# Vision tower block on one core: front half of the next sample run between the heads of the present one

## The chip, the cores and the metric

The kernel runs on one core of one Trainium2 chip. The metric is device time in microseconds (us) from one launch to its end. Before the change two runs took 6684.24 and 6710.91 us, with a median of 6697.57 us. Times in the text that carry no unit are us.

The engines are called PE (TensorE), DVE (VectorE), ACT (ScalarE), POOL (GpSimd) and SP (SyncE, which issues the transfers). PEld is TensorE's weight load. A "record" is one line of the trace; a float32 matmul leaves two records there, a float32r or bfloat16 matmul one.

## The reference, cut to what matters

32 samples, each 64 channels x 256 positions x 4; after the token mixer each is 256 rows of 256 values, and a class row is put in front (257 rows).

```python
# token mixer, per sample (q, k, v are 64x64 projections of the raw sample, per head of 4)
ew = exp(w_bias * local_mask); ek = exp(k)
y = sigmoid(q) * (ew @ (ek * v)) / (ew @ ek)
h = layernorm(y @ out_w + out_b + x) * ln_g + ln_b
# attention, 16 heads, 16 wide q and k, 64 wide v
t = layernorm(concat(cls, h))
q, k, v = l2norm(t @ Wq), l2norm(t @ Wk), l2norm(t @ Wv)      # per head
attn = square(relu(q @ k.T))
out = tanh_norm(attn @ v)                                      # tanh(|o|) * o / |o|
h = concat(cls, h) + out @ Wout
# then a latent attention and a mixture of experts over all rows (not touched by the change)
```

## The kernel before, in words

`build` runs stages one after another: `load_constants`, `mixer_and_attention` (all 32 samples), `class_tokens`, `latent_attention`, and then the experts. Only the first two change; the others take over one tile (`QT` is allocated in `latent_attention` afterwards, and not by `build`).

In `mixer_and_attention` each engine has its own program, and the programs meet at semaphores. Nothing reorders them: the order of the work is the order in which the code is written. Each engine runs a loop over the samples, and one sample goes through its stages in a row:

- **Mixer.** DVE spreads the raw sample (`tensor_copy(x2)`, line 534). PE projects it (lines 678 to 684), ACT takes exponentials, PE forms the two mixes with `ewT` (line 692), DVE takes the reciprocal of the denominator (line 545), PE adds bias, residual and output projection in bank 5 (lines 697 to 706), and DVE makes two layer norms, with the roots on POOL (`power`, line 64).
- **Projections.** PE turns the rows (line 713) and projects q and k (line 719) and v (line 725). ACT squares all of them, DVE sums the squares per head and forms reciprocal roots by Newton steps (`inverse_root`, lines 71 to 81). q and k are then scaled (line 579), split into a high and a low part (`hl`, ACT line 471, DVE and POOL line 420), turned by PE in float32r (line 737) and copied into `QT` and `KTr` (ACT line 477). A head's 16 values become 64 rows this way. v is scaled by DVE into `V` (line 601).
- **Attention.** The work goes by units: `u` is half of the keys (128) for a pair of heads. `sim(u)` (line 754) is two float32r matmuls of 64 rows that run side by side in the array, ACT takes relu (line 486), DVE multiplies relu by the raw product in PSUM (`prob`, line 614), and `values(u)` (line 764) is two float32 matmuls of 64 columns each, side by side. Once per pair the class row enters with one float32 matmul (line 814, `v.vcls_bd`), and `square_sums` (line 772) sums the squares of an output pair with two matmuls whose moving side has 8 columns.
- **Output.** Norms of the outputs, their tanh, a scale per head, which PE turns (line 780) and spreads over the rows as a high and a low part (lines 792 and 793), DVE's scaling (line 646), and the output projection (line 799, 16 float32 matmuls per sample) in bank 5; DVE adds the residual (line 670). Then SP stores the rows, and only then does DVE begin the next sample's line 534.

So PE waits for DVE and ACT in the mixer, the norms and the output, while in the attention PE is always fed.

## Time and the profile before

| what | value |
|---|---|
| runs | 6684.24 and 6710.91 us, median 6697.57 |
| profiled execution, its own time | 6671.73 us |
| span of the profiled execution | 6670.0 us |
| mean granted TensorE clock | 0.696 of full speed |
| PE busy | 77% of the span, 23484 records |
| DVE, ACT, POOL busy | 43%, 27%, 11% |
| samples' copies (line 534), 32 of them | 67.0 to 3272.6 us |

The span runs from the first to the last instruction. The first 67 us are constants; the 32 samples last to 3377 us; all behind that is code that the change leaves alone. The copies of line 534 are (3272.6 - 67.0) / 31 = 103.4 us apart. The profile is one execution; the granted clock says which part of TensorE's 2.4 GHz was granted in a stretch: 1.0 is 2.4 GHz, 0.5 is 1.2 GHz.

### The profile page before, as it was taken

How to read it: one execution, taken by the hardware profiler on the slowest of the kernel's cores; microseconds unless marked ns; L12 is line 12 of the kernel's file. 1: busy time of each engine (PE TensorE's matmuls, PEld its weight loads, DVE VectorE, ACT ScalarE, POOL GpSimd, SP SyncE). 2: the span in 40 equal slices, each digit the busy share in tenths (PEclk: the TensorE clock that was granted, in tenths of full speed). 3: DMA queues.
4: the chain of work that ended last, by engine and by line, in shares of the span. 5: the costliest groups of instructions: out<-in, count | busy, mean ns of one | idle time of the engine just before them, and what ended most of it. 6: DMA issues, size and time to landing. Idle time of an engine off the chain costs nothing. (4 is left out here: it accounts for less than half of the span.)

```text
span 6670.0 us, 76169 instructions
## 1 busy us (share of the span) xinstructions
PE 5105.2 (77%) x23484; PEld 3231.9 (48%) x23485; DVE 2858.4 (43%) x7538; ACT 1831.1 (27%) x5049; POOL 729.7 (11%) x630
## 2 busy tenths in 40 slices
PE   5888888887888878888838889889888862217887
PEld 3454454545545545445415555555555532216776
DVE  3444444444444444444415444544544542213333
ACT  1222222222222222222203333333333331002332
POOL 1000000000000000000050000000000002222333
PEclk7766766667666676676757776776766765559999
DMA  1000000000000000000000000000000021113333
GB/s 39 9 9 5 9 5 9 9 5 9 9 5 9 5 9 9 5 9 5 6 7 12 15 14 10 14 14 13 11 14 14 10 74 58 54 42 60 57 57 55
DMA packets 104402, 131.16 MB, mean 20 GB/s; under 512 B 13698, under 2 KB 84995, under 8 KB 104372
## 3 DMA queue, kind: packets, MB, share of 16 engines
q1 hardware_dynamic: 78404, 95.67, 4.8%
q0 software_dynamic: 25968, 35.15, 3.1%
q8 instruction: 12, 0.20, 0.0%
q14 instruction: 18, 0.15, 0.0%
HBM read 67.00 MB, written 63.76 MB: 20 GB/s over the span
## 5 line engine op out<-in xcount | busy, mean ns | idle before, releaser
L614 DVE TENSOR_TENSOR PR<-psA,R 128x516 f32<-128x516 f32 x512 | 352.4, 693 | 634.7 <-ACT R L486 633.8
L1155 ACT ACTIVATE m_P<-psC,m_nmax 128x129 f32<-128x129 f32 (+1 forms) x1024 | 421.2, 419 | 624.0 <-DVE m_nmax L1239 621.1
L764 PE MATMUL psA<-PR,V 128*64 128x258 f32 x2048 | 568.8, 662 | 0.9
L486 ACT ACTIVATE R<-psA 128x516 f32<-128x516 f32 x512 | 304.7, 601 | 735.8 <-PE psA L754 732.3
L1347 PE MATMUL psC<-ident,m_P 128*128 128x128 f32 x1536 | 402.6, 391 | 68.5 <-ACT m_P L1155 68.5
L1232 DVE COPY m_PT<-psC 128x256 f32<-128x256 f32 (+1 forms) x512 | 284.6, 556 | 391.2 <-PE psC L1347 390.8
L1359 PE MATMUL psC<-m_PT,m_V 128*16 128x128 f32 x3072 | 360.0, 359 | 12.5 <-DVE m_PT L1232 12.5
L799 PE MATMUL psA<-wout,OT 128*128 128x256 f32 x1024 | 362.8, 531 | 0.0
L1347 PEld LDWEIGHTS psC<-ident,m_P 128*128 128x128 f32 x1536 | 226.0, 189 | 239.2 <-ACT m_P L1155 124.6
L64 POOL TENSOR_TENSOR rstd<-rstd,inv_root 128x2 f32<-128x2 f32 x64 | 44.5, 695 | 2601.3 <-DVE rstd L528 2601.3
L1656 PE MATMUL psR<-identd,d_tn 128*128 128x128 f32 x130 | 31.1, 426 | 387.9 <-DVE d_tn L1583 387.9
L1239 DVE TENSOR_REDUCE m_nmax<-psC 128x2 f32<-128x258 f32 (+1 forms) x512 | 285.0, 557 | 96.3 <-PE psC L1335 89.5
L754 PEld LDWEIGHTS psA<-QT,KTr 64*128 64x128 f32 x1024 | 143.2, 283 | 356.8 <-issue 305.3
L814 PE MATMUL psA<-pcl,vcls_bd 16*128 16x258 f32 x512 | 309.5, 704 | 4.9 <-DVE pcl L609 4.6
L799 PEld LDWEIGHTS psA<-wout,OT 128*128 128x128 f32 x1024 | 279.7, 280 | 63.8
L754 PE MATMUL psA<-QT,KTr 64*128 64x258 f32 x1024 | 285.4, 565 | 1.3 <-DVE V L601 1.3
L772 PEld LDWEIGHTS psA<-kmask,osq 128*128 128x128 f32 x1024 | 236.9, 321 | 74.8 <-issue 74.8
L764 PEld LDWEIGHTS psA<-PR,V 128*64 128x64 f32 x2048 | 156.0, 205 | 230.1 <-issue 119.7
L1793 POOL DMA_INDIRECT out_rows<-e_y,e_dest x137 | 212.1, 1548 | 449.6 <-DVE e_y L1852 233.0
L772 PE MATMUL psA<-kmask,osq 128*128 128x8 f32 x1024 | 261.2, 366 | 0.0
L1331 PE MATMUL psC<-m_KT,QT 64*128 64x130 f32 (+1 forms) x1024 | 243.9, 474 | 0.0
L737 PE MATMUL psA<-ident_r,hl 128*128 128x128 f32 x1024 | 127.9, 312 | 132.3 <-DVE hl L420 132.3
(369 smaller groups left out, 9258.9 us busy)
## 6 DMA issues: line engine op xcount, KB each, us to landing
e_x<-xg SPq DMA_DIRECT2D x143, 129.0 KB, 2.5
xraw<-in_x SPq DMA_DIRECT2D x64, 256.0 KB, 3.8
d_x<-xs SPq DMA_DIRECT2D x13, 640.0 KB, 4.4
hs<-h SPq DMA_DIRECT2D x32, 256.0 KB, 2.0
m_h<-hs SPq DMA_DIRECT2D x32, 256.0 KB, 2.7
xs<-m_x SPq DMA_DIRECT2D x32, 256.0 KB, 2.2
out_rows<-m_base SPq DMA_DIRECT2D x32, 256.0 KB, 2.4
w_stage<-in_w SPq DMA_DIRECT2D x16, 512.0 KB, 4.9
```

The source lines that it names most:

```text
L486: act.activation(R[:, h % 2], ps[:, b:b + 2, 0:QCOLS], ACT.Relu).then_inc(relu_done, 1)
L614: dve.tensor_tensor(PR[:, h % 3], ps[:, b:b + 2, 0:QCOLS], R[:, h % 2], ALU.mult).then_inc(prob_done, 1)
L754: last = pe.matmul(ps[:, 2 * (u % 2) + hh, 0:QCOLS], KTr[rows, pr, t * P:(t + 1) * P], v.QT[rows, pr, :], start=True, stop=True)
L764: last = pe.matmul(ps[64 * hh:64 * hh + 64, 4 + pr % 2, 0:QCOLS], V[:, t, h * DV:(h + 1) * DV], PR[:, u % 3, hh, :], start=False, stop=Tru ...
L772: last = pe.matmul(ps[:, 6 + pr // 4, t * 8:t * 8 + 8], osq[:, pr % 2, t * P:(t + 1) * P], v.kmask[:, pr % 4, 0:8], start=pr % 4 == 0 and ...
L799: last = pe.matmul(ps[:, 5, t * MODEL:(t + 1) * MODEL], OT[:, pr, t * P:(t + 1) * P], v.wout[:, pr, :], start=pr == 0 and t == 0, stop=pr ...
L814: pe.matmul(ps[:, 4 + pr % 2, 0:QCOLS], v.vcls_bd[:, pr * P:(pr + 1) * P], pcl[:], start=True, stop=False, skip_group_check=True)
L1155: act.activation(PM[:, u % 2, hh, 0:N - 1], ps[:, b + hh, 0:N - 1], ACT.Exp, bias=nmax[:, t, h:h + 1], accum_out=esum[:, t, h:h + 1]).then ...
L1232: dve.tensor_copy(PT[:, u % 2, 0:n], ps[:, 4 + u % 2, 0:n]).then_inc(pT_copied, 1)
L1239: dve.tensor_reduce(nmax[:, t, 2 * hp:2 * hp + 2], ps[:, b:b + 2, 0:KEYS[t] - 1], AX.X, ALU.max, negate=True).then_inc(max_done, 1)
L1347: last = pe.transpose(ps[:, 4 + u % 2, c:c + P], PM[:, u % 2, hh, 1 + jt * P:1 + (jt + 1) * P], v.ident[:])
L1359: pe.matmul(ps[rows, 6 + g // 2, g % 2 * L + t * P:g % 2 * L + (t + 1) * P], V[:, jt, h * DK:(h + 1) * DK], PT[:, u % 2, c:c + P], start=F ...
```

## The change

It has two halves, and is made in `load_constants`, `mixer_and_attention` and the place where tiles are allocated.

**Order.** Each engine's program is now written as functions per step, and one body `sample(i, d, before, more)` runs the attention of sample i, with the mixer and projections of sample i + 1 (`more`) and the output part of sample i - 1 (`before`) between its eight pairs of heads. The loop holds two bodies, since tiles are kept twice (`d` is 0 or 1). `front(0)` runs the mixer and projections of the first sample alone, and `last` the output of the last.

**Arithmetic.** q and k stay as projected. PE writes them turned (weights stationary, tokens moving, line 971), ACT copies them to `qT` and `kT`, and `sim` becomes four float32 matmuls of 32 rows and 256 columns per pair of heads. The rows of a head are chosen by a parity mask in the copy of k. A key's norm goes into the scale of its value row (`vc = vrn * rk`, on POOL), a query's norm into the norm of the output. Gone are `hl`, its turns (line 737), the Newton roots, and the multiply with the class key (line 744). New are small matmuls for the norm sums of q and k and for the class row (`class_products`, `query_sums`). Roots of v and of the outputs are now POOL's `power` on 16 and 32 columns, and POOL scales v. `prob` squares relu's result, which lies in SBUF, and takes one instruction per pair of heads, as relu does. `square_sums` works with 2 columns. The scale's high and low part go into one matmul of 48 rows, the class row into one float32r matmul of 80 rows.

The core of the diff:

```diff
+            def sim(i, d, p):
+                c, m, g = p // 4, p // 2 % 2, p % 2
...
+                need(pe, relu_done, PAIRS * i + p)
+                for t in range(LT):
+                    for hh in range(2):
+                        rows = slice(32 * (2 * g + hh), 32 * (2 * g + hh) + 32)
+                        last = pe.matmul(ps[:, hh, t * L:(t + 1) * L], kT[rows, d, m, c, t * P:(t + 1) * P],
+                                         qT[rows, d, c, :], start=True, stop=True, skip_group_check=True)
+                last.then_inc(sim_done, 1)
...
+            def attend(i, d, p):
+                if p == 0:
+                    pe.wait_ge(p_ready, i + 1)
+                    pe.wait_ge(v_ready, 2 * i + 2)
+                need(pe, ss_done, PAIRS * i + p - 1)
+                pe.wait_ge(prob_done, PAIRS * i + p + 1)
+                pe.matmul(ps[:, 2 + p % 2, 0:QCOLS], v.vcls3[:, p * P:(p + 1) * P], v.pcl[:, d, :], start=True,
+                          stop=False, skip_group_check=True)
...
+            def prob(i, d, p):
+                dve.wait_ge(relu_done, PAIRS * i + p + 1)
+                need(dve, av_done, PAIRS * i + p - 1)
+                dve.wait_ge(acl_done, i + 1)
+                dve.tensor_copy(PR[:, p % 2, :, :, L],
+                                acl[:, d, :, 2 * p:2 * p + 2].rearrange("p t h -> p h t"))
+                dve.tensor_tensor(PR[:, p % 2, :, :, 0:L], R[:, p % 2], R[:, p % 2], ALU.mult).then_inc(prob_done, 1)
...
+            def value_rows(j, e, t):
+                pool.wait_ge(v_lift, 2 * j + t + 1)
+                power(pool, vrn[:, t], vsm[:, t], v.inv_root).then_inc(v_rn, 1)
+                pool.wait_ge(v_rn, 2 * j + t + 1)
+                pool.wait_ge(k_inv, j + 1)
+                pool.tensor_tensor(vc[:, t], vrn[:, t], rk[:, t], ALU.mult).then_inc(v_c, 1)
+                pool.wait_ge(v_c, 2 * j + t + 1)
+                pool.tensor_tensor(V[:, e, t].rearrange("p (g d) -> p g d", d=DV),
+                                   Vr[:, t].rearrange("p (g d) -> p g d", d=DV),
+                                   vc[:, t].unsqueeze(2).to_broadcast([P, HEADS, DV]), ALU.mult).then_inc(v_ready, 1)
...
+            def output_roots(i):
+                pool.wait_ge(o_lift, i + 1)
+                power(pool, orr[:], osm[:], v.inv_root).then_inc(o_rooted, 1)
```

PE's body of one sample (the first half; `before` and `more` are true in the loop):

```diff
+            def sample(i, d, before, more):
+                j = i + 1
+                sim(i, d, 0)
+                if more:
+                    mixer_inputs(j)
+                if before:
+                    square_sums(i - 1, 7)
+                sim(i, d, 1)
+                attend(i, d, 0)
+                if more:
+                    mix_keys(j)
+                sim(i, d, 2)
+                if more:
+                    mix_values(j)
+                attend(i, d, 1)
+                square_sums(i, 0)
...
```

On PE, at the start of the attention (the second and third pair of heads), the kernel before has the following. `KTr`, `QT` are the keys and queries, `PR` the squared products, `V` the values:

```order
L754 MATMUL psA<-QT,KTr 128x258 x2
L814 MATMUL psA<-pcl,vcls_bd 128x258
L761 REGISTER_ALU
L764 MATMUL psA<-PR,V 64x258 x2
L754 MATMUL psA<-QT,KTr 128x258 x2
L761 REGISTER_ALU
L764 MATMUL psA<-PR,V 64x258 x2
L754 MATMUL psA<-QT,KTr 128x258 x2
L772 MATMUL psA<-kmask,osq 128x8 x2
```

At the same place of the loop body the changed kernel has this; `ekv` and `ewT` are the operands of the next sample's mix, and `scs` and `osc` further on belong to the last sample's output:

```order
L1030 MATMUL psA<-qT,kT 128x256 x4
L455 REGISTER_ALU
L1040 MATMUL psA<-pcl,vcls 128x258
L1045 MATMUL psA<-PR,V 64x258 x4
L934 ISA
L929 MATMUL psA<-ewT,ekv 128x256 x4
L455 REGISTER_ALU
L1030 MATMUL psA<-qT,kT 128x256 x4
L929 MATMUL psA<-ewT,ekv 128x256 x4
L1040 MATMUL psA<-pcl,vcls 128x258
L1045 MATMUL psA<-PR,V 64x258 x4
L1052 MATMUL psA<-half,osq 128x2 x2
```

The full-array matmuls of the mix, which stood ahead of the whole attention, now stand between its pairs, and so do the projections and the output projection further down.

On DVE, the kernel before ran units of `prob` one after another (`R` is relu's result):

```order
L609 TENSOR_TENSOR pcl<-psA,rcl 16x258
L612 ISA
L614 TENSOR_TENSOR PR<-psA,R 128x516
L612 REGISTER_ALU
L614 TENSOR_TENSOR PR<-psA,R 128x516
L612 REGISTER_ALU
L614 TENSOR_TENSOR PR<-psA,R 128x516
```

The changed kernel has on DVE, from its second pair of heads on (`den`, `rden` are the next sample's mixer, `onm`, `orn`, `ors` the last sample's output, `orr` is POOL's root):

```order
L760 COPY PR<-acl 128x4
L762 TENSOR_TENSOR PR<-R 128x4x256
L693 REGISTER_ALU
L695 SCALAR_TENSOR_TENSOR den<-eq,psA 128x512
L698 RECIPROCAL rden<-den 128x512
L782 TENSOR_TENSOR onm<-oss,orr 128x32
L783 TENSOR_SCALAR orn<-orr 128x32
L785 TENSOR_TENSOR ors<-orn,rq 128x32
L757 REGISTER_ALU
L760 COPY PR<-acl 128x4
L762 TENSOR_TENSOR PR<-R 128x4x256
```

The reciprocal and the wait for POOL's root now stand between two squarings of the attention, where nothing of another stage stood before.

## Rows read from the trace of the kernel before

**Rows 1.** Constants, samples: us; busy PE, PEld, DVE, ACT, POOL; PEclk; DMA share; GB/s.
```profile
0.00:67.67 67.67, 10.99 (x35) 3.94 (x36) 17.90 (x32) 3.43 (x5) 21.37 (x32) 0.84 0.29 87
67.67:3377.00 3309.33, 2772.62 (x9984) 1644.71 (x9984) 1517.15 (x3871) 824.52 (x1728) 139.12 (x128) 0.67 0.03 7
```
**Rows 2.** The same view, stages of one sample (1620.6 to 1724.5 us).
```profile
1643.00:1656.00 13.00, 12.21 (x24) 4.81 (x23) 6.12 (x16) 2.98 (x4) 0.23 (x1) 0.85 0.00 0
1656.00:1666.00 10.00, 5.77 (x42) 4.74 (x44) 8.52 (x19) 6.26 (x13) 2.73 (x2) 0.72 0.00 0
1666.00:1706.00 40.00, 39.82 (x138) 18.75 (x138) 14.64 (x35) 13.78 (x32) 0.00 (x0) 0.50 0.00 0
1706.00:1716.00 10.00, 10.00 (x35) 8.45 (x34) 4.48 (x21) 0.88 (x3) 0.00 (x0) 0.55 0.00 0
```
**Rows 3.** Timeline of PE, one pair of heads: start, us, line.
```profile
1671.10 1.22 PE L814 MATMUL psA<-pcl,vcls_bd 16*128 16x258 f32 x2
1672.24 1.13 PE L764 MATMUL psA<-PR,V 128*64 128x258 f32 x4
1673.30 0.58 PE L754 MATMUL psA<-QT,KTr 64*128 64x258 f32 x2
1673.82 1.13 PE L764 MATMUL psA<-PR,V 128*64 128x258 f32 x4
...
1675.38 1.02 PE L772 MATMUL psA<-kmask,osq 128*128 128x8 f32 x4
1676.33 0.79 PE L814 MATMUL psA<-pcl,vcls_bd 16*128 16x258 f32 x1
```
**Rows 4.** Busy time by stretch, where one other sample enters its attention.
```profile
530.00:534.00 4.00, 3.87 (x15) 1.50 (x15) 1.89 (x3) 1.12 (x3) 0.00 (x0) 0.58 0.00 0
534.00:540.00 6.00, 6.00 (x20) 2.85 (x20) 2.09 (x3) 2.80 (x7) 0.00 (x0) 0.50 0.00 0
```
**Rows 5.** Timeline of PE, work met at the full clock.
```profile
529.39 0.39 PE L754 MATMUL psA<-QT,KTr 64*128 64x258 f32 x2 [0.17 <-DVE V L601]
529.82 0.70 PE L814 MATMUL psA<-pcl,vcls_bd 16*128 16x258 f32 x2
...
1616.20 3.72 PE L799 MATMUL psA<-wout,OT 128*128 128x256 f32 x16
...
1621.22 0.39 PE L678 MATMUL psA<-biasr,ones_bf 96*128 96x512 bf16 x1 [1.31 <-DVE x L534]
...
1623.40 1.03 PE L684 MATMUL psA<-x,wq_bd 128*128 128x256 f32 x4
...
1625.17 3.72 PE L692 MATMUL psA<-ewT,ekv 128*128 128x256 f32 x16 [0.75 <-ACT ekv L452]
...
1628.95 1.05 PE L701 MATMUL psA<-ident,x 128*128 128x128 f32 x8
...
1648.18 7.03 PE L725 MATMUL psA<-wv,xT 128*128 128x512 f32 x16
```
**Rows 6.** DVE and ACT groups by form: busy, mean ns, idle before.
```profile
L614 DVE TENSOR_TENSOR PR<-psA,R 128x516 f32<-128x516 f32 x512 | 352.4, 693 | 634.7 <-ACT R L486 633.8
L545 DVE RECIPROCAL rden<-den 128x512 f32<-128x512 f32 x32 | 107.3, 3353 | 1.1
...
L579 DVE TENSOR_TENSOR qkn<-psA,rn 128x1024 f32<-128x1024 f32 x32 | 39.2, 1225 | 1.1
...
L463 ACT ACTIVATE sq<-psA 128x1024 f32<-128x1024 f32 x64 | 64.8, 1013 | 77.1 <-PE psA L725 77.1
```
**Rows 7.** POOL's powers and its overlap with DVE, groups by form.
```profile
L64 POOL TENSOR_TENSOR c_rn<-c_ss,inv_root 1x48 f32<-1x48 f32 x1 | 8.0, 8013 | 33.0 <-DVE c_ss L268 33.0
...
L64 POOL TENSOR_TENSOR b_nrm<-b_ssum,root 128x256 f32<-128x256 f32 x1 | 41.1, 41126 | 72.1 <-DVE b_ssm L910 72.1
...
L420 POOL TENSOR_TENSOR hl<-qkn,hl 128x512 fp32r<-128x512 f32 x64 | 94.7, 1500 | 509.2 <-ACT hl L471 509.2
...
L420 DVE TENSOR_TENSOR hl<-qkn,hl 128x512 fp32r<-128x512 f32 x64 | 80.4, 1294 | 19.5 <-ACT hl L471 19.5
```

More of the change, by code:

```diff
@@ new lines, in _, with pairs @@
+            dve.tensor_reduce(v.parity[:], v.ind8[:].rearrange("p (e q) -> p e q", e=2), AX.X, ALU.add)
+            dve.wait_ge(cls_sum, 1)
+            def pairs(x):
+                return x.rearrange("p (c q e) -> p c e q", c=2, q=4)
+            for k in range(KT):
+                for r in range(3):
+                    dve.tensor_copy(v.wkc[:, k, 32 * r:32 * r + HEADS].rearrange("p (c e q) -> p c e q", c=2, e=2),
+                                    pairs(sums[:, k]))
+                dve.tensor_copy(v.wqc[:, k].rearrange("p (c e q) -> p c e q", c=2, e=2), pairs(sums[:, 2 + k]))
@@ L447, in _, with mixer @@
+            front(0, 0)
+            samples(pool, sample, lambda i, d: output_roots(i))
         @block.scalar
         def _(act):
-            with act.Fori(0, nb) as i:
-                act.wait_ge(kvq_done, i + 1)
+            def mixer(j):
+                act.wait_ge(q_done, j + 1)
+                act.activation(eq[:], ps[:, BQ, :].rearrange("p (a n) -> p a n", a=2), ACT.Exp, bias=v.nbq[:],
+                               scale=-1.0).then_inc(eq_done, 1)
                 for t in range(LT):
-                    act.activation(ekv[:, t, 0], ps[:, t, :].rearrange("p (a n) -> p a n", a=2)[:, :, 0:P],
+                    act.wait_ge(kv_done, LT * j + t + 1)
+                    act.activation(ekv[:, t, 0], ps[:, BK0 + t, :].rearrange("p (a n) -> p a n", a=2)[:, :, 0:P],
@@ new lines, in last @@
+            def last(i, d):
+                keep_sums(i, d, 7)
+                output_norms(i, d)
+                output_scale(i, d)
+                output_scale_turned(i)
+                split_scale(i)
+                for m in range(4):
+                    scale_outputs(i, d, m)
+                result(i)
+            dve.sem_inc(h2_stored, 1)
+            dve.memset(osc[:], 0.0)
+            dve.memset(PR[:], 0.0).then_inc(cleared, 1)
+            dve.wait_ge(cleared, 1)
+            front(0, 0)
@@ L672, in _, with mixer_inputs @@
+            samples(dve, sample, last)
         @block.tensor
         def _(pe):
-            with pe.Fori(0, nb) as i:
-                pe.wait_ge(x2_ready, i + 1)
+            def mixer_inputs(j):
+                pe.wait_ge(x2_ready, j + 1)
+                need(pe, v_sq, 4 * j)
+                need(pe, q_sq, j)
+                need(pe, q_lift, j)
+                for hp in range(2):
+                    last = pe.matmul(ps[:, BQ, hp * 256:hp * 256 + 256], v.wq_bd[:], x2[:, hp, :], start=True, stop=True)
+                last.then_inc(q_done, 1)
@@ L837, in class_tokens, with last @@
+            def last(i, d):
+                square_sums(i, 7)
+                turn_scale(i, False)
+                spread_scale(i, 0, False)
+                spread_scale(i, 1, False)
+                project_outputs(i, 0)
+                spread_scale(i, 2, False)
+                project_outputs(i, 1)
+                spread_scale(i, 3, False)
+                project_outputs(i, 2)
+                project_outputs(i, 3)
+            front(0)
+            samples(pe, sample, last)
 def class_tokens(nc, v, a, nb):
```

1055 lines of the change are left out of this document (647 added, 408 removed).

## The prediction

> **What bounds the kernel now.** I read the busy time by stretch first, to see what a sample costs: the 32 samples take 3309 us, or 103.4 us each, and PE is busy for 2773 of them at a mean clock of 0.67; DVE is busy for 1517, ACT 825, POOL 139 [rows 1]. So even all of DVE's work is 47 us a sample, and the other engines' could lie beside PE's. Next I took one sample by stages. In the attention PE is busy 39.82 of 40.00 us, at a clock of 0.50, the lower of its two levels (1.2 GHz), and that is so for all of the 40 us [rows 2]. In the projections it is busy 12.21 of 13 us at 0.85, and before the attention, while DVE, ACT and POOL norm, split and turn, it is busy for only 5.77 of 10 us [rows 2]. The other gaps lie in the mixer and the output. The rest of the program, from 3377 us on, is not touched.
>
> Two things bound a sample: PE's work in order of the chain (PE idles (3309 - 2773) / 32 = 17 us a sample), and the clock, which is low for the longest stage although PE never rests in it. Then I read the timeline for single steps. A pair of heads takes 1676.33 - 1671.10 = 5.23 us: 1.14 for the class row, twice 1.06 for the values, twice 0.52 for the products, 0.95 for the square sums [rows 3].
>
> **What the clock does.** The rows show that work which fills the array raises it: the projections, full 128 x 128 float32 matmuls without a gap, are at 0.85 on the mean [rows 2], and their second part runs at 0.43 a record, 512 columns twice, which is the full level [rows 5]; the output projection begins in a stretch of 0.55 [rows 2], and the second half of it takes 0.22 a record, full again [rows 5]. Attention does not hold it: one sample entered its attention at the full clock and had 0.58 in the next 4 us and 0.50 behind that, with PE busy throughout [rows 4]. Its matmuls fill 64 rows, 64 columns side by side, 16 rows, or move 8 columns. This is what the change meets most: it puts a block of full-array matmuls, 1.7 to 3.5 us long, between any two pairs of heads. In the changed order the longest run without one is about two attention steps, some 4 to 5 us, where the kernel before has 40.
>
> The Trainium skill (TensorE: Matmul & The Clock Gate, section Why this matters for your kernels) ties the full level to a TensorE kept busy without gaps. The trace disagrees for the attention: 39.82 of 40 us busy, and 0.50 [rows 2]. By the skill's rule the changed kernel, busier than before, would stay at the full level throughout; that is the first rival below.
>
> **The change part by part, PE, per sample.** First at the full clock.
>
> 1. Full-array work that is only moved. Inputs of the mixer 1624.43 - 1621.22 = 3.2 us (the last record of line 684 ends at 1624.43). Line 692: 16 records in 3.72, 0.22 each, 3.5. Residual and its bias 1.3 (line 701 takes 1.05, its 2 bias matmuls the rest). Output of the mixer, 8 records of 0.22, 1.8. The turn of the rows 0.5. q, k and v: 24 records at 7.03 / 16 = 0.43 each, 10.3 (q and k now have 16 records of half the columns, the same sum). Output projection, 32 records at 0.22, 7.0 [rows 5]. Sum 27.6.
> 2. Attention steps, 8 of them. Products: formerly two float32r matmuls side by side took 0.52 at 1.2 GHz and 0.43 at 2.4 [rows 3, 5]; halving the stream saves 0.09 to 0.11, so about 0.3 of either is a fixed cost. Now there are two such pairs, but in float32, each two records of 0.22 plus 0.3: 1.5 per step (2.3 at the low clock; before 1.04). No row has 32 rows of the array: the ends are 0.9, with the fixed part hidden as in line 799, and 2.4, with the two not side by side. I take 1.5, the form nearest to line 754. Values: 1.06 is 2 x 0.43 streaming plus 0.2, so twice 0.63 at the full clock, 1.25. Class row: one float32r pass, as line 754, 0.4 (0.5 low), where float32 took 1.14. Square sums: 0.95 low, 4 records at 0.11 to 0.13 plus the switch, 0.7. Sum 3.85 full, 5.9 low; times 8, 31 and 47. At the low clock a step thus costs more than the 5.23 before.
> 3. New: 12 small matmuls of norm sums and class products, 24 records at 0.11 to 0.13 as line 701 [rows 5] (0.22 to 0.24 low, as line 772 [rows 3]), and two of 80 columns, 0.9: 3.5 full, 7 low. Gone: 32 turns of line 737 and 8 matmuls of line 744, most of the 5.77 busy us [rows 2].
> 4. Turn and spread of the scale (8 matmuls instead of 16) with switches 2 (3 low). About ten more switches between full and partial array, 3.
> 5. Waits left. I walked the four programs side by side. DVE holds PE at three places: `prob(0)` stands behind the last sample's sums, which PE only makes after the mixer's inputs, 1 us; `turn_scale` needs the reciprocal, 3.35 us [rows 6], a squaring and four small operations, 0.6; a block of the output projection waits 0.5 for a scaled pair. Products, relu (1.0 for 1024 elements, as line 463) and the next products share two banks, but another block lies between. Of these 2 us, 1 is already in the switches. v of the next sample is ready 10 us after its last projection, and is asked for 15 us after it.
>
> Sum: 27.6 + 31 + 3.5 + 2 + 3 + 1 = 68 us at the full clock. At the low clock the same list is 54 + 47 + 7 + 3 + 2 = 113 us, above the 103.4 of before. So the whole gain hangs on the clock and on the waits, and both ends of its price are known: 68 and 113.
>
> **Which value I take.** Each sample has at least four full-array runs of 3.4 us at the full clock, 6.8 at the low one (mixer output with the first output block, output blocks 3 and 4, keys with the first values, the mixer's inputs), which is the kind of work that raised the clock before [rows 2, 5]. It can fall at the sample's seam (square sums, query sums, first products) and where square sums, turn and products follow each other. I take one fifth of the work at the low level: 0.8 x 68 + 0.2 x 113 = 77 us a sample.
>
> Beside PE: DVE has now about 32 us a sample (8 squarings of 1.2 instead of 16 products of 0.69 [rows 6], no Newton steps, no `hl`), ACT 25. POOL is new as a worker. `power` took 8.01 us for 48 columns and 41.1 for 256 [rows 7], so 0.16 to 0.17 a column: 16 columns are 2.7 to 3.1, 32 are 5.3 to 5.6. With two of the first, one of the second, two scalings of 1024 elements (1.5 us for 512 in line 420 [rows 7], so up to 3 each) and small things it has 22 us. The 5.6 us root is asked for behind prob(1) and the reciprocal, some 9 us after it starts: hidden. If that cover goes, it costs up to 5.6.
>
> **The sum.** Constants 67.7 + 8 (one more round trip of a store and a load, 16 DVE and 7 POOL operations; 2 to 14). First front, nothing beside it, 50 (before 45 from copy to attention, less the turns, plus POOL's roots). 31 x 77 = 2387. The last sample's attention with the output of the one before, 45, and its own output, 18. That ends at 2576 instead of 3377. Rest 6670.0 - 3377 = 3293. Span 5869, execution 1.7 more, 5871. The profiled execution of before, 6671.7, lies 0.4% under its median of 6697.6, so 5871 stands for 5893 in the median.
>
> **Rivals.**
> - The clock stays full: 68 a sample, 31 x 9 = 279 less, 5614. For it: full-array blocks at every step. Against: attention lets it fall within 4 us [rows 4], and the seam is as long.
> - POOL and DVE get in each other's way. `prob` now reads R twice from SBUF, before it read PSUM and R; while POOL ran line 420, DVE's line 420 took 1294 ns for 512 elements, where 516 take 693 in line 614 [rows 6, 7]. POOL is at work for 22 us a sample. If a squaring waits for a running power, prob(0) and prob(1) stand behind the 5.6 us root, attend(0) is late by 5.4 us, and the value scalings add 3: 9 us a sample, 31 x 9 = 279 more, 6172. The Trainium skill (SBUF — State Buffer, section Who interferes with whom) says that a DVE operation with two SBUF inputs and a GpSimd one that reads SBUF exclude each other for the whole instruction. By that rule it would be this rival; line 420's two rows fit it and do not prove it.
> - Slower than before. The blocks do not raise the clock, because the products in 32 rows and the waits dilute them: all at 1.2 GHz, 113 a sample, 31 x 36 = 1116 more, 7009. Against it: runs of 6.8 us at the low level with nothing else in them. It decides from 103 us a sample on, that is with 78% of the work at the low level.
> - Products of 32 rows do not run side by side: 0.87 more per step, 7 us a sample at the full clock, 31 x 7 = 217 more, 6110. The pairs of line 754 do (0.52 for both [rows 3]), so I hold it unlikely.
>
> **How the numbers follow.** My forecast, 77 a sample, 5893, has 0.55, with 5750 to 6080 as its own range (72 to 83). Clock always full 0.2. POOL and DVE, or other waits of that size, 0.13; side by side failing 0.02; half of the work low (90, 6296) 0.04; slower 0.06. The range reaches from 5600 to 6400. A measurement of this kernel tells 2% from no change. Below 6563 is faster by over 2%: 0.91. Slower by over 2%, above 6832, is the last rival: 0.06. Between: 0.03.
>
> **What would show it.** The copies of x2 would be 77 us apart in the loop and not 103. The granted clock over the samples would be about 0.85 to 0.9, low only in short stretches at the seam; PE busy over 90%. `sim` would take 1.5 us at the full clock, POOL's 32-column power 5.6. I am wrong if the clock over the samples is under 0.7, if PE waits more than 5 us a sample (then the row that names DVE or POOL as releaser tells which rival), or if the four matmuls of `sim` start one after another.

## The result: 5530 us, and the profile after

| what | before | after |
|---|---|---|
| median of the runs | 6697.57 us | 5529.97 us (5513.70 and 5546.24) |
| profiled execution; its span | 6671.7; 6670.0 us | 5513.7; 5512.0 us |
| mean granted clock, whole span | 0.696 | 0.802 |
| one sample in the loop | 103.4 us | 66.4 us |

The ratio is 0.826, with a 95% interval of 0.813 to 0.838: 17% faster. The prediction said 5893, with a range from 5600 to 6400. It had the direction, and the two things that bound a sample; the time lies below the range.

Busy time by stretch of the kernel after: constants; the first front alone; body of sample 0; 29 bodies; the last two bodies and the last output (columns as in [rows 1], which answer to it).

```profile
0.00:80.50 80.50, 9.19 (x18) 2.16 (x19) 22.86 (x47) 3.43 (x5) 28.36 (x42) 0.81 0.33 80
80.50:121.90 41.40, 30.37 (x118) 21.25 (x120) 15.02 (x34) 9.69 (x19) 8.40 (x10) 0.79 0.05 13
121.90:179.60 57.70, 54.49 (x280) 35.72 (x278) 25.67 (x58) 23.12 (x43) 18.34 (x15) 0.85 0.04 10
179.60:2108.10 1928.50, 1805.85 (x9342) 1228.99 (x9340) 919.06 (x2147) 670.08 (x1276) 564.07 (x406) 0.91 0.04 12
2108.10:2242.00 133.90, 117.68 (x576) 78.88 (x572) 52.77 (x131) 36.96 (x70) 33.99 (x19) 0.82 0.01 4
```

The long row is the loop: 1928.5 / 29 = 66.5 us a sample, where [rows 1] had 103.4. PE is busy for 94% of it, and the clock is 0.91 where it was 0.67. The samples end at 2242 and not 3377. The rest of the program takes 5512 - 2242 = 3270 us, before 3293. Nothing there was changed. PE's granted clock over it was 0.74 here and 0.72 before, and the same code took 3225 us (at 0.75) to 3308 us (at 0.71) in the profiled executions of the kernels below. So a difference of some tens of us between two whole times is not yet one of the samples; the spacing of the samples is the surer measure.

The same view for 4 us pieces of one sample, in answer to [rows 2] and [rows 4]:

```profile
1047.00:1051.00 4.00, 2.55 (x18) 1.78 (x18) 3.25 (x11) 1.41 (x2) 2.54 (x1) 0.91 0.00 0
1051.00:1055.00 4.00, 4.00 (x18) 2.36 (x16) 0.80 (x2) 0.66 (x2) 2.87 (x1) 0.67 0.00 0
1055.00:1059.00 4.00, 4.00 (x26) 2.67 (x26) 3.96 (x4) 1.02 (x1) 0.00 (x0) 1.00 0.00 0
1059.00:1063.00 4.00, 2.92 (x26) 2.39 (x24) 3.22 (x12) 0.78 (x3) 0.00 (x0) 1.00 0.00 0
1063.00:1067.00 4.00, 4.00 (x21) 2.27 (x17) 1.43 (x3) 1.59 (x3) 0.00 (x0) 0.61 0.00 0
1067.00:1071.00 4.00, 4.00 (x12) 3.26 (x13) 0.82 (x3) 0.09 (x1) 0.00 (x0) 0.53 0.00 0
```

The clock is no longer low for a stage, but for two patches. Each comes behind 4 us in which PE waited and had mostly small work (busy 2.55 and 2.92 of 4 us), and ends with a block of full-array matmuls. The next sample, which begins with a longer wait (below), has a third patch, on the mixer's inputs (0.57 from 1111.5 to 1115.5 us); the two kinds take turns.

The timeline of PE shows the blocks, in answer to [rows 3] and [rows 5] (start, us, line; the last bracket is the idle time before and who ended it):

```profile
1050.03 0.36 PE L1040 MATMUL psA<-pcl,vcls 80*128 80x258 f32 x1 [1.45 <-DVE PR L762]
1050.31 1.99 PE L1045 MATMUL psA<-PR,V 128*64 128x258 f32 x8
1052.23 2.69 PE L929 MATMUL psA<-ewT,ekv 128*128 128x256 f32 x8
1054.85 1.13 PE L1030 MATMUL psA<-qT,kT 32*128 32x256 f32 x8
1055.91 1.99 PE L929 MATMUL psA<-ewT,ekv 128*128 128x256 f32 x8
1057.55 0.47 PE L1040 MATMUL psA<-pcl,vcls 80*128 80x258 f32 x1
1057.95 1.09 PE L1045 MATMUL psA<-PR,V 128*64 128x258 f32 x8
1058.97 0.61 PE L1052 MATMUL psA<-half,osq 128*128 128x2 f32 x4
1059.44 0.38 PE L945 MATMUL psA<-biasr,ones_bf 96*128 96x256 bf16 x2
```

From start to start, at the full clock: the four products 1055.91 - 1054.85 = 1.06 us, the class row 0.40, the values 1.02, the square sums 0.47. At the low clock the values take 1050.31 to 1052.23, 1.92. So a step of the attention is 2.95 us at the full clock, where [rows 3] had 5.23 at the low one.

The waits of PE in the 29 bodies (line, waited for, us in total, times, longest):

```profile
PE psA L1040 <- DVE PR L762: 43.4, 29, 1.6
PE psA L916 <- DVE x L684: 35.1, 29, 2.1
PE psA L1061 <- DVE osc L791: 29.7, 29, 1.3
PE psA L1080 <- DVE OT L804: 14.5, 29, 0.5
```

Together 122.7 / 29 = 4.2 us a sample, before 17. Groups of DVE and POOL by form in the same stretch, in answer to [rows 6, 7]:

```profile
L762 DVE TENSOR_TENSOR PR<-R 128x1024 f32<-128x1024 f32 x232 | 283.6, 1222 | 0.0
L65 POOL TENSOR_TENSOR vrn<-vsm,inv_root 128x16 f32<-128x16 f32 x58 | 167.8, 2894 | 8.0 <-POOL pcl L514 4.8
L65 POOL TENSOR_TENSOR orr<-osm,inv_root 128x32 f32<-128x32 f32 x29 | 157.0, 5413 | 148.0 <-DVE osm L776 148.0
L525 POOL TENSOR_TENSOR V<-Vr,vc 128x1024 f32<-128x1024 f32 x58 | 114.0, 1966 | 4.5
L684 DVE COPY x<-xraw 128x512 f32<-128x512 f32 x29 | 38.9, 1340 | 3.3 <-issue 3.3
```

POOL's powers take what was worked out (2.89 and 5.41), its scaling 1.97 and not up to 3. One row is odd: the copy of the raw sample takes 1340 ns on the mean.

### The profile page after: what moved, and what is told of

The parts are those of the page before. It is cut to its first block and busy times, and to the rows that moved or that the text cites. A ratio compares the mean times of both kernels' runs of the same rounds, so it can differ in the third digit from the quotient of the medians.

```text
span 5512.0 us, 73809 instructions
## 1 busy us (share of the span) xinstructions
PE 4288.3 (78%) x23788; PEld 2925.6 (53%) x23789; DVE 2356.9 (43%) x6050; ACT 1743.5 (32%) x4729; POOL 1222.8 (22%) x960
## 5 line engine op out<-in xcount | busy, mean ns | idle before, releaser
L598 ACT ACTIVATE R<-psA 128x1024 f32<-128x1024 f32 x256 | 262.0, 1023 | 674.2 <-PE psA L1030 674.2
L1045 PE MATMUL psA<-PR,V 128*64 128x258 f32 x2048 | 335.2, 456 | 0.0
L762 DVE TENSOR_TENSOR PR<-R 128x1024 f32<-128x1024 f32 x256 | 312.9, 1222 | 0.0
L1030 PE MATMUL psA<-qT,kT 32*128 32x256 f32 x2048 | 292.6, 403 | 0.6 <-ACT R L598 0.6
L1080 PE MATMUL psA<-wout,OT 128*128 128x256 f32 x1024 | 249.0, 392 | 16.6 <-DVE OT L804 16.6
L992 PE MATMUL psA<-wv,xT 128*128 128x512 f32 x512 | 250.1, 612 | 0.0
L1680 PE MATMUL psC<-m_KT,m_QT 64*128 64x130 f32 (+1 forms) x1024 | 237.4, 461 | 0.0
L1030 PEld LDWEIGHTS psA<-qT,kT 32*128 32x128 f32 x2048 | 176.2, 185 | 100.1 <-issue 85.4
L65 POOL TENSOR_TENSOR orr<-osm,inv_root 128x32 f32<-128x32 f32 x32 | 174.3, 5446 | 159.9 <-DVE osm L776 159.9
L1680 PEld LDWEIGHTS psC<-m_KT,m_QT 64*128 64x128 f32 x1024 | 127.4, 246 | 146.8 <-issue 135.4
```

The source lines that it names most:

```text
L598: act.activation(R[:, p % 2], ps[:, 0:2, :].rearrange("p a (t n) -> p a t n", t=LT), ACT.Relu).then_inc(relu_done, 1)
L762: dve.tensor_tensor(PR[:, p % 2, :, :, 0:L], R[:, p % 2], R[:, p % 2], ALU.mult).then_inc(prob_done, 1)
L992: last = pe.matmul(ps[:, bank, :], xT[:, k, t * P:(t + 1) * P], v.wv[:, k, half * 512:(half + 1) * 512], start=k == 0, stop=k == KT - 1)
L1030: last = pe.matmul(ps[:, hh, t * L:(t + 1) * L], kT[rows, d, m, c, t * P:(t + 1) * P], qT[rows, d, c, :], start=True, stop=True, skip_grou ...
L1045: last = pe.matmul(ps[64 * hh:64 * hh + 64, 2 + p % 2, 0:QCOLS], V[:, d, t, n * DV:(n + 1) * DV], PR[:, p % 2, hh, t, :], start=False, sto ...
L1080: last = pe.matmul(ps[:, BOUT, t * MODEL:(t + 1) * MODEL], OT[:, m % 2, p % 2, t * P:(t + 1) * P], v.wout[:, p, :], start=p == 0 and t == ...
```

## The experiments

The theory from the two traces was: the order of the work fills PE's waits and keeps the clock, and nearly all of the gain comes from it; the arithmetic by itself gains nothing; what is left over the full-clock sum are waits and the low patches, which belong together. The first rival was that the new arithmetic is the gain. Below, "before" is 6656 to 6679 us, its median in the run's own comparison; every ratio and interval is against it.

### The arithmetic without the order

The changed kernel with all steps of a sample in a row, as before: the body of each engine has no `more` and `before` parts between the pairs.

```diff
-            def sample(i, d, before, more):
-                j = i + 1
-                sim(i, d, 0)
-                if more:
-                    mixer_inputs(j)
...
+            def sample(i, d, more=True):
+                sim(i, d, 0)
+                for p in range(1, PAIRS):
+                    sim(i, d, p)
+                    attend(i, d, p - 1)
+                    if p >= 2:
+                        square_sums(i, p - 2)
...
+                if more:
+                    front(i + 1)
```

> The changed arithmetic with the order of before: attention, output, then mixer and projections of the next sample, nothing interleaved. Theory (the interleaved full-array blocks are what keeps the clock up): the attention falls back to a granted clock of 0.50, its step of a pair takes about 5.2 us (products 1.9, class row 0.5, values 1.92, square sums 0.88) and not 3.0, and a sample about 98 us: 41 front, 42 attention, 15 output. In all 5530 + 31 x 32 = 6520 us. Rival (interleaving only fills idle time, the new arithmetic holds the clock by itself): the step stays at 3.0, a sample is 80 us, in all 5950 us.

Measured: 6809 us, ratio 1.022 (1.013 to 1.030). The new arithmetic alone is 2% slower than before. Its attention is at 0.50: products 2.01 us, class row 0.51, values 1.92, square sums 0.95, 5.4 a step, where before had 5.23. The theory had the step nearly right (5.2), but 6520 as the time. From the end of a sample's attention to the first matmul of the next one it is 26.6 us and not 15: the output part is late by itself now, as the view of waits shows (1000 to 2000 us, 9 samples):

```profile
PE psA L971 <- DVE osc L753: 66.6, 9, 7.4
PE psA L874 <- DVE xn L690: 53.2, 9, 5.9
```

The first wait holds POOL's 5.4 us root, which nothing covers in this order. So the whole 17%, and 2% more, is due to the order, on top of the new arithmetic; the new order with the old arithmetic was not run. What the order gives can be read from the loop of this kernel, which has the same matmuls as the changed one (columns as in [rows 1]):

```profile
300.00:3500.00 3200.00, 2491.21 (x9547) 1603.44 (x9547) 968.04 (x2193) 696.31 (x1309) 616.11 (x419) 0.66 0.02 7
```

Its samples are 108.1 us apart, with PE busy for 84.1 of them and idle for 24.0; the changed kernel has 66.4, 62.2 and 4.2. So of the 41.7 us a sample that the order saves, about half (19.8) are waits of PE that it fills, and the other half (21.9) is the same matmuls run at a clock of 0.91 in place of 0.66. Against the kernel before, which was idle for 17 us and busy for 86.6, the new arithmetic alone saves 2.5 us of PE's work and adds 7 of waits, which is why it is slower.

### Added full-array work in the kernel before

Eight more matmuls behind each of the pairs 0 to 6, whose result nobody uses; in the second kernel they fill 16 rows of the array instead of 128. In both, the filler writes into bank 7, where the class products and the norm sums of the second group stand, so the values of the output part change; the instructions are those of before plus the filler.

```diff
                     if pr >= 1:
                         square_sums(pr - 1)
+                    if pr < PAIRS - 1:
+                        for _ in range(8):
+                            pe.matmul(ps[:, 7, 384:512], v.half1[:], v.ident[:], start=True, stop=True,
+                                      skip_group_check=True)
```

> The kernel before, with 8 more full-array float32 matmuls of 128 columns behind each of the first 7 pairs of heads; their result is not used, so this is added work only. They take 16 records of 0.11 = 1.8 us at the full clock, 3.5 at the low one. Theory (full-array blocks between pairs are what keeps the clock up): the attention leaves 0.50, a pair costs about 3.3 us at the full clock in place of 5.23, plus 2.0 for the filler, so a sample changes by 7 x (5.3 - 5.23), about nothing, and the time is 6660 to 6720 although PE does 450 us more work. Rival (the clock of the attention is not moved by such blocks): still 0.50, 7 x 3.6 = 25 us a sample more, 32 x 25 = 800 more, 7460.

> The same 8 added matmuls per pair, of the same shape in columns (128 x 128) but with 16 rows of the array filled instead of 128: the control for the filler. Theory (it is filling the array that raises the clock, not the number of matmuls or the absence of gaps): clock in the attention stays 0.50, the time is 7460. Rival (any longer block of matmuls raises it): as the full filler, 6660 to 6720.

Measured: 6542 us with the full filler, ratio 0.982 (0.977 to 0.986), and 7411 with the narrow one, 1.112 (1.107 to 1.117). A kernel that was bound by PE became 1.8% faster though PE had 1.96 x 7 = 13.7 us more to do in each sample; no change had been expected, as a pair was taken to cost 5.3 us with its filler. PE's timeline of the first one, where a sample enters its attention:

```profile
1717.14 3.72 PE L826 MATMUL psA<-ident,half 128*128 128x128 f32 x16
1720.78 0.70 PE L814 MATMUL psA<-pcl,vcls_bd 16*128 16x258 f32 x2
...
1722.00 0.39 PE L754 MATMUL psA<-QT,KTr 64*128 64x258 f32 x2
1722.31 0.66 PE L764 MATMUL psA<-PR,V 128*64 128x258 f32 x4
...
1723.68 2.03 PE L826 MATMUL psA<-ident,half 128*128 128x128 f32 x16
1725.64 0.70 PE L814 MATMUL psA<-pcl,vcls_bd 16*128 16x258 f32 x2
```

The first filler takes 3.64 us, at the low level; behind it everything is at the full one, and stays there for the rest of the attention: a pair with its filler takes 1725.64 - 1720.78 = 4.86 us, less than the bare pair's 5.23. The control, on the same view:

```profile
1647.01 1.06 PE L814 MATMUL psA<-pcl,vcls_bd 16*128 16x258 f32 x2
...
1652.09 3.78 PE L826 MATMUL psA<-ident 16*128 16x128 f32 x16
1655.66 1.06 PE L814 MATMUL psA<-pcl,vcls_bd 16*128 16x258 f32 x2
```

The same number of matmuls, without a gap, and the clock stays low: 1655.66 - 1647.01 = 8.65 us a pair. The clock over the samples is 0.64 with the narrow filler and 0.85 with the full one. What raises the clock here is that the array is filled, not that PE is busy. Only 16 and 128 rows were tried; what a filler in between would do is open.

The same filler in the serial kernel with the new arithmetic, in spare columns of bank 7:

```diff
                     if p >= 2:
                         square_sums(i, p - 2)
+                    for _ in range(8):
+                        pe.matmul(ps[:, BSC, 384:512], v.half1[:], v.ident[:], start=True, stop=True,
+                                  skip_group_check=True)
```

> The new arithmetic in the order of before (6809), with the same 8 full-array matmuls behind each of the first 7 products of a pair. Theory (order brings the clock): an attention step of 5.4 us at 0.50 becomes 2.95 + 2.0 at the full clock, 8 x 2.45 = 19.6 less and 7 x 2.0 = 14 more, 5.6 us a sample, 31 x 5.6 = 174 less than 6809, 6635, with added work. Rival (the gain of the interleaving is the gaps it fills, not the clock): 0.50 stays, 7 x 3.7 = 26 us a sample more, 7610. Half the way in clock gives about 7100.

Measured: 6783 us, 1.018 (1.013 to 1.023), not told apart from the 6809 without it, where 6635 was expected. The clock over the samples rose from 0.66 to 0.82, and a step with its filler takes 4.83 us where the bare one took 5.4; the sample became 1.2 us shorter and not 5.6: the first step and its filler are still at the low level, and the output part waits 7.4 us as before, behind which the clock is low again. The rival, 7610, is out.

### The waits that PE had left

Three edits on the changed kernel. In `copy_early` DVE copies the raw sample (`tokens`) one sample ahead, ahead of the squaring of pair 6, and SP loads it one sample earlier:

```diff
-                if more:
-                    tokens(j)
                 if before:
...
+                if more and ahead:
+                    tokens(i + 2)
                 prob(i, d, 6)
```

In `prob_first` the squaring of pair 0 stands ahead of the last sample's sums:

```diff
+                prob(i, d, 0)
                 if before:
                     keep_sums(i - 1, 1 - d, 7)
                     output_norms(i - 1, 1 - d)
-                prob(i, d, 0)
```

and `three_waits` has both, and the turn and the spread of the scale each one block later on PE:

```diff
-                if before:
-                    turn_scale(i - 1, more)
                 sim(i, d, 3)
                 if before:
-                    spread_scale(i - 1, 0, more)
-                    spread_scale(i - 1, 1, more)
+                    turn_scale(i - 1, more)
                 attend(i, d, 2)
                 square_sums(i, 1)
+                if before:
+                    spread_scale(i - 1, 0, more)
+                    spread_scale(i - 1, 1, more)
```

> The copy of the raw sample (x2) made on DVE one sample ahead, behind the result of the last sample, where POOL is idle, and not at the seam beside POOL's scaling of v. Theory (the copy is held up by POOL, PE waits for it, and the clock falls behind that wait): the copy takes 0.5 us each time, the 35 us of waits of the mixer's inputs go, the low stretch at the seam gets shorter, the samples come 64 us apart: 5450 us. Rival (the clock has nothing to do with that wait): only the waits go, 1.2 us a sample, 5493 us. Second rival: the wait moves to the first attend, which waits for DVE already: within 15 us of 5530.

> On DVE the first squaring of a sample stands ahead of the sums and norms of the last one. Theory (the wait of the first attend, 43.4 us over 29 samples, is only the order on DVE): it goes, 1.5 us a sample, 5484 us; the root on POOL starts 1.4 us later and stays hidden. Rival (the root is on the path): the turn of the scale waits 1.4 us longer instead, 5530 us.

> Both edits together, and PE turns the last sample's scale behind the fourth products and spreads it behind attend 2. Theory (waits of 1.2, 1.5 and 1.0 us a sample go, and the clock gains where PE no longer pauses): 115 us of waits and some 50 of clock, 5370 us, the granted clock over the samples up from 0.91 to 0.95. Rival (the waits come back elsewhere, since DVE and ACT are paced by PE): 5470 us, with the clock as it was.

Measured: 5466 us (0.818, 0.813 to 0.823), 5408 (0.812, 0.809 to 0.815) and 5270 (0.792, 0.788 to 0.796). The last one beats both kernels: a fifth faster than before. The first came out near what was expected with the clock counted in; the other two came out lower than expected (5484 and 5370). All three gave more than the waits that went: 2.7 us a sample for 1.2, 4.3 for 1.5 and 8.3 for 3.7 (table below). In `three_waits` PE waits for one thing only, and over 1550 us of samples it reads:

```profile
PE psA L1091 <- DVE OT L807: 13.3, 27, 0.5
```

```profile
300.00:1850.00 1550.00, 1536.52 (x8597) 1062.73 (x8597) 829.91 (x1979) 613.91 (x1171) 509.62 (x371) 0.98 0.05 14
```

PE is busy for 99% of it, at 0.98.

### A wait put back, at two places

Does a wait cost its own length, or the clock behind it too? `three_waits` with an idle reciprocal on DVE ahead of one squaring, at pair 0 with 512 elements and at pair 7 with 640:

```diff
+                if p == 0:
+                    dve.reciprocal(dly[:, d], one[:])
                 dve.tensor_copy(PR[:, p % 2, :, :, L],
```

> three_waits (5270) with a reciprocal of 512 elements, 3.35 us on DVE, put ahead of the squaring of pair 0. In three_waits the squaring is done 1.9 us before PE asks, so PE waits about 1.4 us per sample there, and nothing else changes. Theory (an idle of PE near the seam also lets the clock fall, which is why removing 1.0 to 1.2 us of wait gave 2.8 and 4.4 us a sample): the sample is 3 to 4 us longer, the clock over the samples 0.95 or less, 31 x 3.5 = 110 more, 5380. Rival (a wait costs its own length): 1.4 x 31 = 43 more, 5313, clock 0.98.

> three_waits with a reciprocal of 640 elements, 4.2 us on DVE, ahead of the squaring of pair 7, which is done 2.7 us before PE asks: PE waits about 1.5 us per sample, behind the projection of the queries. Theory (a short idle behind full-array blocks of 2 to 4 us does not move the clock; it matters where it stands): 1.5 x 31 = 47 more, 5317, clock 0.97 to 0.98. Rival (any idle of this length costs the clock too): 3 to 4 us a sample, 5380, clock 0.95 or less.

Measured: 5311 (0.798, 0.793 to 0.802) and 5379 (0.806, 0.801 to 0.812). Each time the rival's number was the nearer one, though at pair 0 the wait did not come as often as both had assumed. At pair 7 the wait of 1.2 us, 37 in all, costs 108 us. At pair 0, behind the mixer's inputs, the wait came in half of the samples only (300 to 1850 us):

```profile
PE psA L1056 <- DVE ssb L773: 17.7, 13, 1.4
```

That is 0.7 us a sample, or 22 in all. The samples are 0.7 to 0.8 us longer, at a mean clock of 0.98 as before, so here the waits cost about themselves. The medians are 40 us apart, but four runs of `three_waits` alone spread from 5237 to 5295, so they cannot tell 22 from 40. The clock was not untouched either: behind 6 of these 13 waits stands a low stretch that `three_waits` does not have at this place (0.57 from 949 to 953 us, while 1009 to 1013, behind the next wait, is at 1.00); in turn, samples with such a wait have none on the mixer's inputs.

For the wait at pair 7 the groups of PE show where the time goes, first without the wait, then with it (300 to 1850 us):

```profile
L927 PE MATMUL psA<-x,wq_bd 128*128 128x256 f32 x104 | 37.8, 499 | 0.0
L1011 PE MATMUL psA<-ind,qsq 128*128 128x8 f32 x208 | 27.0, 256 | 0.0
```

```profile
L1056 PE MATMUL psA<-pcl,vcls 80*128 80x258 f32 x204 | 96.4, 473 | 30.0 <-DVE ssb L773 30.0
L932 PE MATMUL psA<-x,wq_bd 128*128 128x256 f32 x104 | 46.1, 588 | 0.0
L1016 PE MATMUL psA<-ind,qsq 128*128 128x8 f32 x208 | 33.8, 290 | 0.0
```

Behind the wait of 1.2 us stand the last class row and values, square sums, query sums with 8 columns and the first products, and only then full-array matmuls. Those small ones and the first of the inputs got slower (256 to 290, 499 to 588 ns): the wait made the stretch without full-array work longer.

So a wait just ahead of the seam cost more than twice its length, and one behind the inputs its own. That is no rule of places: `prob_first` took 1.5 us of wait away from this same place behind the inputs and gained 4.3. There, in every other sample, the copy's wait of 2.1 us stood a few us ahead of it; in `wait_at_seam` nothing did. How waits that lie near each other add up in the clock is not shown by these runs.

### POOL's root twice

The 32-column power of the output norms is done a second time, 5.4 us more of POOL in each sample.

```diff
+                power(pool, orx[:], osm[:], v.inv_root)
                 power(pool, orr[:], osm[:], v.inv_root).then_inc(o_rooted, 1)
```

> The changed kernel, with POOL's 32-column power of the output norms done twice, 5.4 us more of POOL per sample. In the trace the root is there 5.07 us before DVE takes it. Theory (POOL is off the path and hidden by the attention): the root is 0.35 us late, 31 x 0.35 = 11 more, 5530 to 5550. Rival (POOL's powers slow DVE's work on SBUF beside them, or the work of both is on the path): up to 5.4 us a sample, 5690.

Measured: 5523 (0.829, 0.825 to 0.833), the same as the changed kernel, and 66.6 us a sample against 66.4. The single root is hidden. The second is hidden in every other sample only: PE's wait for the turned scale, first in the changed kernel, then here (300 to 1850 us), is

```profile
PE psA L1061 <- DVE osc L791: 23.3, 23, 1.1
PE psA L1063 <- DVE osc L793: 42.6, 23, 3.1
```

The 0.8 us a sample of added wait does not show in the time; the mean clock is 0.92 in place of 0.91, so the low patches became a little shorter. The rival, up to 5.4 us a sample, is out. POOL's powers don't slow DVE's squaring beside them: 1223 ns here, 1222 in the changed kernel.

### What makes four products take 1.07 us

First the loops of `sim` are exchanged; then all four matmuls read the same 32 rows.

```diff
-                for t in range(LT):
-                    for hh in range(2):
+                for hh in range(2):
+                    for t in range(LT):
```

```diff
-                        rows = slice(32 * (2 * g + hh), 32 * (2 * g + hh) + 32)
+                        rows = slice(32 * (2 * g), 32 * (2 * g) + 32)
```

> The changed kernel with the two loops of sim exchanged, so that the two matmuls of the same 32 rows follow each other and the two halves of the rows no longer alternate. Theory (the four products cost 1.06 us because two and two run side by side, 4 slots of 0.21 plus 0.2 once per block; the prediction paid 0.3 twice): at most the middle two can still overlap, so sim takes 1.5 to 1.9 at the full clock, 0.45 to 0.85 more per step, 3.6 to 6.8 us a sample, 31 x 5 = 160 more, 5640 to 5740. Rival (the order of issue does not matter, or they were never side by side): 1.06 as before and 5530.

> The changed kernel with both heads' products read from the same 32 rows (the second head of a pair takes the first one's keys and queries, so the values of the attention change; the number and shape of the matmuls do not). It asks what makes four matmuls take 1.07 us, since exchanging the loops did not change it. Theory (two matmuls run at once because they lie on different rows of the array, and PE finds the pair by itself in either order): now nothing can run at once, 8 records x 0.21 + 0.2 = 1.9 us at the full clock, 0.85 more per step, 6.8 us a sample, 31 x 6.8 = 210 more, 5740. Rival (it is the two records of one float32 matmul of 32 rows that run at once, whatever the other rows do): 1.07 and 5530.

Measured: the exchange changed nothing, 5508 us (0.826, 0.819 to 0.834), and my theory for it fell. The same rows gave 5648 (0.846, 0.843 to 0.848), and one sample 70.8 us instead of 66.4. One block of products of each on PE's timeline:

```profile
1056.94 1.14 PE L1030 MATMUL psA<-qT,kT 32*128 32x256 f32 x8
1058.01 0.50 PE L1073 MATMUL psA<-scs,ind 48*128 48x256 f32 x2
```

```profile
1047.93 1.99 PE L1030 MATMUL psA<-qT,kT 32*128 32x256 f32 x8
1049.85 0.50 PE L1073 MATMUL psA<-scs,ind 48*128 48x256 f32 x2
```

1.07 and 1.92 us: two products run at once when they lie on different rows, in either order of the loops, and one after another when they don't. Eight records of 0.21 plus 0.2 are 1.9, four such slots plus 0.2 are 1.07, as expected. The 7 us a sample that the prediction's fourth rival gave to it are 8 x 0.85 = 6.8; 4.4 arrived, as the longer products give DVE more time: PE's waits fell from 4.2 to 1.7 us a sample. How PE pairs matmuls that do not stand next to each other in the program, the trace doesn't show; that stays open.

## Why the prediction was wrong, point by point

The runs let a sample be taken apart. The work at the full clock is the sample's time, less PE's waits, less half of the time at the low level (half, since work takes about twice as long there, as the values with 1.92 and 1.02 us; at a mean clock c the low share of time is 2 x (1 - c); the clock is the mean over the samples of the loop; waits are taken to lie at the full level, which holds in these kernels and not in the serial ones):

| kernel | sample | waits | clock | lost to the clock | work at full clock |
|---|---|---|---|---|---|
| predicted | 77 | 1 | - | 9 | 67 |
| after | 66.4 | 4.2 | 0.912 | 5.8 | 56.4 |
| copy_early | 63.7 | 3.0 | 0.934 | 4.2 | 56.5 |
| prob_first | 62.1 | 2.7 | 0.952 | 3.0 | 56.4 |
| three_waits | 58.1 | 0.5 | 0.981 | 1.1 | 56.5 |
| wait_at_seam | 58.8 | 1.2 | 0.979 | 1.2 | 56.4 |
| wait_at_last_pair | 60.8 | 1.7 | 0.959 | 2.5 | 56.6 |

The last column is the same in the six kernels that ran, within 0.2 us, so the division holds.

**What bounds the kernel, what the clock does: right.** Full-array blocks between the pairs raise the clock; the filler shows it by itself, and the control that it is not busy time. The Trainium skill's rule (TensorE: Matmul & The Clock Gate, section Why this matters for your kernels), which ties the full level to an engine kept busy, was rightly set aside: the trace disagrees, with 0.61 and 0.53 in two stretches above in which PE was busy for 4.00 of 4 us and just ahead of which it had stood for 1.07 us.

**Item 2, attention steps: the step that failed.** It had 3.85 us for a step at the full clock; 2.95 was measured. Products: predicted 1.5 with ends 0.9 and 2.4, measured 1.06. Values: 1.25, measured 1.02. Square sums: 0.7, measured 0.47. The class row was right, 0.40. The error is in the fixed parts. For the products I read 0.3 us of fixed cost per pair of matmuls side by side from 0.52 us at the low clock and 0.43 at the full one. But the 0.43 of [rows 5] held a wait: line 814 began at 529.82 because DVE's `pcl` (line 609) ended at 529.76. Fed without a gap, the same pair takes 1722.31 - 1722.00 = 0.31 in `before_filled`, so the fixed part is 0.1 and not 0.3. For the values I paid 0.2 twice, and it comes once per block of one kind: four records take 0.59 us in `before_filled`, eight take 1.02 here. The rows did not say what eight in a row take, and I took the costlier reading. For the square sums I added a switch to four records of 0.12, and none shows. 8 x 0.9 = 7.2 us a sample. The Trainium skill (TensorEngine Tiling (Array Packing), section Key Properties) says that changing the tiling mode drains the engine; one fixed part per block agrees with that, though no run here separates the drain from other fixed costs.

**Item 4, switches: counted twice.** The prediction has 3 us for "about ten more switches" on top of steps whose measured durations hold them. From start to start the full-array blocks take what item 1 gave (27.2 measured in `three_waits`, 27.6 predicted), item 3 is 3.6 (3.5). With item 2 and small things that is 67 - 56.4 = 10.6 us a sample too much. The low sum, 113, leaves out one of its list's terms: with the turn and spread at 3, ten switches at 3 and a wait of 1 it is 115, which moves the forecast by 0.4 us a sample.

**Item 5, waits: too small.** 2 us, of which 1 was counted; 4.2 were measured. `prob(0)` had 1 and cost 1.5, the turn 0.6 and cost 1.0, the output block 0.5 and cost 0.5. One was not named at all: the copy of the raw sample at the seam, 1.2 us on the mean, 0.2 and 2.1 in turn. DVE can begin it only behind the last sample's query sums, and PE asks for it at once.

**The value between the ends: too careful.** One fifth of the work at the low level, 9 us; it was 5.8 us, a tenth of the work. The places were right: behind the seam, and where the turn, products and square sums follow each other.

**The sum.** Less work 10.6, less lost to the clock 3.2, more waits 3.2: 10.6 us a sample, times 31 = 329. The first front took 41.4 and not 50, constants 80.5 and not 75.7, the rest 3270 and not 3293, by its clock. Together 329 + 8.6 - 4.8 + 23 = 356, where 5871 - 5514 = 357.

**The rivals.** The clock always full (68 a sample, 5614): the clock was not, yet the time came out lower still, because the list was. Slower: out, the low level has a tenth of the work and not 78%. Products not side by side: out, they are, and a kernel in which they are not takes 5648. POOL and DVE: its mechanism was given the wrong victim. The squaring reads R twice from SBUF and takes 1222 ns on the mean of 232, also beside POOL's 5.4 us power (two begin at 1048.66 and 1050.53 us and take 1.22 each, while a power runs from 1048.46 to 1053.87). But DVE's copy of the raw sample is held up by POOL's scaling of v, as the timelines of DVE and POOL show:

```profile
1108.20 2.09 DVE L684 COPY x<-xraw 128x512 f32<-128x512 f32 x1 [0.23 <-issue]
```

```profile
1107.92 1.90 POOL L525 TENSOR_TENSOR V<-Vr,vc 128x1024 f32<-128x1024 f32 x1
```

POOL's ends at 1109.82, the copy at 1110.29, 0.47 later, which is about what the copy needs by itself. One sample earlier the copy begins 0.12 us ahead of POOL's scaling; then it is the copy that is quick, and POOL's multiply takes 2.17 us and not 1.90:

```profile
1043.14 0.52 DVE L684 COPY x<-xraw 128x512 f32<-128x512 f32 x1
```

```profile
1043.26 2.17 POOL L525 TENSOR_TENSOR V<-Vr,vc 128x1024 f32<-128x1024 f32 x1
```

So the mean of 1340 ns is of two kinds of sample, about 0.5 and 2.1 us. In `copy_early` the same copy stands where POOL has nothing to scale:

```profile
L687 DVE COPY x<-xraw 128x512 f32<-128x512 f32 x26 | 17.3, 667 | 142.2 <-DMA xraw<-in_x 142.2
```

667 ns against 1303 over the same 1650 us of the changed kernel. The Trainium skill (SBUF — State Buffer, section Who interferes with whom) says that a copy in its two-port mode and a GpSimd instruction exclude each other for the whole instruction, and that the one which issues first has its way. The trace agrees with both: 2.09 us for the copy that began second, 0.52 for the one that began first. The same section says that a DVE operation with two SBUF inputs contends with a GpSimd one that reads SBUF. Beside `power` the trace disagrees: 1.22 us for the squaring, as otherwise. Beside the scaling of v no squaring stood in the stretch read, so for that pairing it is open.

**The range.** It ended at 5600, the clock-always-full case. That bound was taken from the clock alone, though the terms of item 2 had ends of their own (0.9 for the products): with these, 31 x 8 x 0.6 = 150 us less, it would have held the time.

## What to carry to other kernels

When the profile shows PE busy and its clock at 0.50, look for full-array work that can be put between the small matmuls. Here the order alone took the new arithmetic from 6809 to 5530 us, half of it by the clock and half by waits that it filled, while the same arithmetic in the old order was 2% slower than before. Then take away the waits that are left: near stretches of small matmuls they cost 2.2 to 2.9 times their length in four of five edits here, and about their own in one. When durations are added up, take them from start to start of blocks, make sure that the next block was not waiting for something, pay fixed parts once per block, and let the range hold the bounds of the terms, not only of the mechanism.

## What the runs showed of the hardware that I had not expected

- Added work made a kernel faster: 13.7 us more of full-array matmuls in each sample, 1.8% less time. The same count with 16 rows filled: 11% more.
- Two float32 matmuls of 32 rows ran at once in either order of issue; on the same rows, 1.92 us instead of 1.07.
- A DVE copy of 512 elements took 0.67 us alone and 2.09 when it began 0.28 us behind POOL's scaling; when it began 0.12 us ahead it took 0.52, and the scaling 2.17 in place of 1.90. A squaring of 1024 elements took 1.22 beside POOL's power.
- Code that no edit touched took 3225 to 3308 us from one kernel's profiled execution to another's, with a mean clock of 0.75 to 0.71 in it.
